# Last stage of a graph network: spreading the senders' values without diagonals, and the low rows of the table made by GpSimd

## The reference, cut to what matters

```python
def _L1_gnn_ref(x, edge, W, a):
    h = x @ W
    src, dst = (edge[0], edge[1])
    s = h @ a[:f_out]
    t = h @ a[f_out:]
    logit = s[src] + t[dst]
    e = jnp.exp(-jax.nn.leaky_relu(logit, ALPHA))
    rowsum = jax.ops.segment_sum(e, src, num_segments=n)
    msg = e[:, None] * h[dst]
    h_prime = jax.ops.segment_sum(msg, src, num_segments=n)
    h_prime = h_prime / rowsum[:, None]
    return jax.nn.relu(h_prime)
...
x = _layernorm(x + _L1_gnn_ref(x, edge_index, L1_gnn_W, L1_gnn_a), axis=-1)
```

## Time and profile before

| | |
|---|---|
| time, median of three runs | 2623.73 us (2621.55 to 2624.15) |
| time of the profiled execution | 2622.26 us |
| span of its instructions | 2620.5 us |
| busy: PE, DVE, ACT, POOL | 93%, 75%, 50%, 22% of the span |
| last stage: first DMA issue, end of the span | 1706.8 us, 2620.5 us |
| mean granted clock of PE | 0.972 |

### The profile page before, as it was taken

The page is one execution under the profiler, slowest core; times in us unless marked ns, Lnnn a source line. Parts: engine busy times, 40 slices in busy tenths (PEclk is TensorE's granted clock), DMA queues, the critical chain, the costliest instruction groups (busy, mean ns, idle before and its releaser), DMA issues. The chain is left out here.

```text
span 2620.5 us, 46932 instructions
## 1 busy us (share of the span) xinstructions
PE 2425.1 (93%) x16048; PEld 1966.7 (75%) x16048; DVE 1954.9 (75%) x3244; ACT 1318.5 (50%) x2190; POOL 578.7 (22%) x629
## 2 busy tenths in 40 slices
PE   3899969999999999959898889889999999999996
PEld 2566647777777777736565556579999999999996
DVE  5899966666666666637576566589999898989896
ACT  3222338888888888814433334355434334343432
POOL 4698960000000000024243324100001010101010
PEclk9999989999999999979999999989999999999998
DMA  3111102223223222250202111166464545454543
GB/s 99 36 46 44 44 18 120 117 106 132 106 109 129 106 121 117 106 173 29 71 29 71 57 57 43 57 149 145 94 124 90 117 89 124 89 121 89 120 92 71
DMA packets 405991, 239.92 MB, mean 92 GB/s; under 512 B 326288, under 2 KB 397584, under 8 KB 399568
## 3 DMA queue, kind: packets, MB, share of 16 engines
q1 hardware_dynamic: 397536, 228.12, 32.0%
q10 hardware_dynamic: 7056, 6.43, 0.7%
q0 software_dynamic: 1248, 3.41, 0.5%
HBM read 48.38 MB, written 110.84 MB: 61 GB/s over the span
## 5 line engine op out<-in xcount | busy, mean ns | idle before, releaser
L1792 PE MATMUL d_acc<-d_rows_high,d_weights_high 128*128 128x258 f32 x2401 | 682.8, 284 | 6.1 <-DVE d_weights_low L1668 6.1
L1793 PE MATMUL d_acc<-d_rows_low,d_weights_high 128*128 128x258 f32 x2401 | 678.6, 283 | 0.0
L1794 PE MATMUL d_acc<-d_rows_high,d_weights_low 128*128 128x258 f32 x2401 | 678.2, 282 | 0.0
L1422 PE MATMUL b_pagg<-x_parts,b_counts 128*128 128x512 f32 x2401 | 656.4, 410 | 0.5 <-ACT b_counts L1463 0.5
L1742 ACT CAST d_weights_high<-d_weights 128x896 fp32r<-128x896 f32 x343 | 323.4, 945 | 500.9 <-PE d_acc L1794 293.3
L1422 PEld LDWEIGHTS b_pagg<-x_parts,b_counts 128*128 128x128 f32 x2401 | 423.7, 189 | 74.4 <-ACT b_counts L1463 1.1
L1792 PEld LDWEIGHTS d_acc<-d_rows_high,d_weights_high 128*128 128x128 f32 x2401 | 455.3, 190 | 10.2 <-DVE d_weights_low L1668 6.0
L1793 PEld LDWEIGHTS d_acc<-d_rows_low,d_weights_high 128*128 128x128 f32 x2401 | 455.3, 190 | 2.2 <-issue 2.2
L1794 PEld LDWEIGHTS d_acc<-d_rows_high,d_weights_low 128*128 128x128 f32 x2401 | 455.1, 190 | 0.0
L1107 DVE TENSOR_TENSOR b_lo_hot<-b_nodes,b_ends 128x1024 bf16<-128x1024 f16 x392 | 270.9, 691 | 210.9 <-PE b_pcounts L1433 210.5
L1668 DVE TENSOR_TENSOR d_weights_low<-d_weights,d_weights_high 128x896 fp32r<-128x896 f32 x343 | 373.1, 1088 | 52.8 <-ACT d_weights_high L1742 51.2
(11 more groups left out here) (160 smaller groups left out, 2790.4 us busy)
## 6 DMA issues: line engine op xcount, KB each, us to landing
edge_counts<-b_counts SPq DMA_DIRECT2D x49, 1568.0 KB, 5.1
node_table<-u_table SPq DMA_DIRECT2D x7, 903.0 KB, 6.3
qx<-in_x SPq DMA_DIRECT2D x49, 128.0 KB, 2.0
x_table<-x_tile ACTq DMA_DIRECT2D x49, 128.0 KB, 1.7
agg<-b_sums SPq DMA_DIRECT2D x49, 128.0 KB, 4.5
u_x<-x_table SPq DMA_DIRECT2D x7, 896.0 KB, 8.2
u_agg<-agg SPq DMA_DIRECT2D x7, 896.0 KB, 10.1
u_x<-in_x SPq DMA_DIRECT2D x7, 896.0 KB, 5.1
```

Of the source, the lines that this page charges most:

```text
L1422: last = nc.tensor.matmul(pagg[:, o, :], ca[:, o, hi, :], x1_parts[:, hi].rearrange("p m d -> p (m d)"), start=(hi == 0), stop=(hi == TILE ...
L1792: nc.tensor.matmul(acc[:, r, 0:HT], a, high[:, t, :], start=(t == 0), stop=False)
L1793: nc.tensor.matmul(acc[:, r, 0:HT], a, low[:, t, :], start=False, stop=False)
L1794: return nc.tensor.matmul(acc[:, r, 0:HT], b, high[:, t, :], start=False, stop=(t == TILES - 1))
```

## The change

DVE no longer makes diagonals. The spread of four tiles of senders' values is now four matmuls of 128 columns: the stationary operand is one column of `st` repeated 128 times, the moving operand is the identity. PE no longer waits for DVE there, only for ACT to have kept the spread before.

`set_ones` and `rows_low` move from DVE to POOL. `rows_low` becomes two instructions: the staged row times `t_scale`, written in place, and then that minus `high`. The second waits for the first on the new semaphore `scaled`. POOL's queue holds all 49 rows ahead of its loop over the inverse roots. DVE's queue in the first group keeps `weigh` and `weights_low` alone.

```diff
@@ vector
-                    dve.wait_ge(ones_ready, 1)
-                    for q in range(FIRST):
-                        diagonals(q)
-                    set_ones(0)
-                    for m in range(ROWS_AHEAD - 1):
-                        rows_low(m)
...
                             if t >= 1:
                                 weights_low(J, t - 1)
-                            if not finish:
-                                if late_spread(t):
-                                    diagonals(late_spread(t))
-                                if t + ROWS_AHEAD < TILES and (t + ROWS_AHEAD) % GROUP == 0:
-                                    set_ones((t + ROWS_AHEAD) // GROUP)
-                                if t + ROWS_AHEAD - 1 < TILES:
-                                    rows_low(t + ROWS_AHEAD - 1)
@@ gpsimd
                     nc.gpsimd.memset(ones[:], 1.0).then_inc(ones_ready, 1)
+                    pool.wait_ge(ones_ready, 1)
+
+                    def set_ones(g):
+                        pool.wait_ge(tab_in[g % 2], 16 * (g // 2) + 16)
+                        nc.gpsimd.tensor_copy(staged[g % 2][:, :, D], ones[:, 0:GROUP]).then_inc(one_set, 1)
+
+                    def rows_low(m):
+
+                        row = staged[m // GROUP % 2][:, m % GROUP, :]
+                        pool.wait_ge(high_ready, m + 1)
+                        nc.gpsimd.tensor_tensor(row, row, t_scale[:, m:m + 1].broadcast_to([P, HT]), ALU.mult).then_inc(scaled, 1)
+                        pool.wait_ge(scaled, m + 1)
+                        nc.gpsimd.tensor_tensor(low[:, m, :], row, high[:, m, :], ALU.subtract).then_inc(low_ready, 1)
+
+                    set_ones(0)
+                    for m in range(TILES):
+                        if (m + ROWS_AHEAD) % GROUP == 0 and (m + ROWS_AHEAD) // GROUP < GROUPS:
+                            set_ones((m + ROWS_AHEAD) // GROUP)
+                        rows_low(m)
@@ tensor
                     def spread_sources(q):
-                        pe.wait_ge(diag_ready, q + 1)
                         if q >= 1:
                             pe.wait_ge(s_ready, q)
                         at = spread_cols(q)
-                        nc.tensor.matmul(acc[:, GROUP, 0:at.stop - at.start], ones[:], diag[:, q % 2, 0:at.stop - at.start],
-                                         start=True, stop=True).then_inc(spread, 1)
-
-                    pe.wait_ge(ones_ready, 1)
+                        for t in range(q * per, min(TILES, (q + 1) * per)):
+                            col = t % per * P
+                            last = nc.tensor.matmul(acc[:, GROUP, col:col + P], c["st"][:, t, 0:1].broadcast_to([P, P]), c["ident"][:],
+                                                    start=True, stop=True)
+                        last.then_inc(spread, 1)
+
```

More of the change, by code:

```diff
@@ L1486, in weigh_and_sum @@
         t_cap, t_scale = sb("d_t_cap", [P, TILES]), sb("d_t_scale", [P, TILES])
-        diag, ones = sb("d_diag", [P, 2, 512]), sb("d_ones", [P, P])
+        ones = sb("d_ones", [P, P])
         cnt = sb("d_counts", [P, GROUP, cols], F16)
@@ L1504, in weigh_and_sum @@
             kit.sem("d_" + s) for s in ("added", "stats", "mean", "var", "rstd", "ready"))
-        ones_ready, diag_ready, spread, s_ready, exp_t = (
-            kit.sem("d_" + s) for s in ("ones_ready", "diag_ready", "s_spread", "s_ready", "exp_t"))
-        one_set, high_ready, low_ready = (kit.sem("d_" + s) for s in ("one_set", "rows_high", "rows_low"))
+        spread, s_ready, exp_t = (kit.sem("d_" + s) for s in ("s_spread", "s_ready", "exp_t"))
+        ones_ready, one_set, high_ready, scaled, low_ready = (
+            kit.sem("d_" + s) for s in ("ones_ready", "one_set", "rows_high", "rows_scaled", "rows_low"))
         tab_in = [kit.sem(f"d_table_loaded{k}") for k in range(2)]
```

## The result

The changed kernel takes 2637.04 us (median of five runs, 2634.74 to 2639.23) against 2623.73 us for the kernel before (median of five, 2621.55 to 2624.59). The ratio is 1.0055, with a 95% interval of 1.0041 to 1.0068: slower by 13.3 us. The forecast was 2644 us, with a range of 2631 to 2662.

What follows compares the result with a forecast made beforehand. PE bounds the first group, DVE close behind. DVE's 101.0 + 95 x 0.54 = 152.3 us moves the group's end from 1852.0 to 1872.5, a 20.5 us loss: 2642.8 on the profiled execution, 2644.2 forecast, range 2631 to 2662.

Steps and rivals of the forecast that it cites:

- PE is the bound, DVE close behind: First group before the change: PE needs 2.52 us a tile, 5.90 for two with a spread; DVE about as much.
- The start, at most 1.2 us: Group's start: first `weigh` no earlier, first `weights_low` about 2.1 us behind it instead of 3.31; worth at most 1.2 us.
- The spreads on PE, taken at nothing: Four matmuls replacing one on PE: eight weight loads hide, a spread still costs 0.86 us, nothing added.
- the rival that they become PE's bound: Spreads' weight loads don't hide on PE: 12 us more than the main case, 2656 us; chance 0.05.
- POOL and DVE take turns: First group: each new POOL instruction waits for DVE's instruction in hand, then holds up the next; a tile takes 3.14 us.
- 0.54 us for each: DVE's loss per POOL row instruction in the first group; 95 of the 98 stand between DVE instructions.
- a multiply that holds DVE half as long: Low variant of the main case, from the multiply's repeated column: a tile takes 2.87 us, the kernel 2634 us.
- Seven blocks ahead, which covers a few us: SP's table-tile loads wait for `low_ready` with transposes behind them; their lead of seven blocks was said to cover a few us.
- POOL's rows hidden: Rival: PE stays the bound if a POOL instruction costs DVE under 0.23 us; 2622.5 us, not slower; chance 0.13.
- POOL holds DVE for its whole instruction: Rival: each POOL instruction costs DVE 0.725 us, 17.6 us more than the main case: 2662 us; chance 0.05.
- PE's clock falls for the whole group: Rival: PE's waits lower its clock, products 0.22 us apart in the first group; about 2735 us; chance 0.04.
- PE waits in nearly every tile: Sign in the first group: PE should wait for `weights_low` or the low rows in nearly every tile.

Runs made afterwards that it cites:

- the first experiment: The changed kernel with `set_ones` and `rows_low` put back into DVE's queue as one instruction, the spreads staying new: 2619.93 us, ratio 0.9984 against the kernel before.

## Why the prediction was right, and where it was off

**PE is the bound, DVE close behind: right.** With 23.6 us of rows kept and 10.7 us of diagonals taken from DVE, the first experiment's group is as long as before.

**The start, at most 1.2 us: nothing came of it.** The first `weigh` still waits for its transposed counts, as predicted. The first `weights_low` comes 1720.01 - 1717.09 = 2.9 us after it, not 2.1, since POOL already takes its turns there.

**The spreads on PE, taken at nothing: right.** 0.89 us for 0.86; the rival that they become PE's bound is refuted by the first experiment.

**POOL and DVE take turns: right, but 0.54 us for each was too much.** This is the mis-sized term. In the undisturbed tiles, 2.87 to 2.98 us, the cost is (2.92 - 2.06) / 2 = 0.43 us, and in all 35.6 us were added to DVE's lines instead of 51.3: by 0.43 that is 83 instructions' worth, not 95. In the trace 85 of POOL's 98 row instructions are in hand when a DVE instruction of the group starts; the others ran ahead of the group or while DVE stood. The prediction named a multiply that holds DVE half as long as the way to a tile of 2.87 us and to 2634 us. The tiles come close to that, but by another split. In the timeline above `weigh` lasts 1.50 us behind a multiply, 0.35 over its 1.15, and `weights_low` 1.63 behind a subtraction, 0.54 over its 1.09; around 1836 us, where the pairs lie the other way round, the multiply costs 0.41 and the subtraction 0.38. Alone the multiply is the shorter of the two, 0.61 us against 0.74; that its repeated column is the reason was not tried. The counts of turns bear the mechanism out: one for a row costs nothing in the whole, two cost about 10 us, three 38 us more, and with a second input in PSUM the collision is gone. (POOL's instruction in the earlier trace rows is L749, not the L747 of the earlier trace rows; its own median is 0.728 us, so nothing hangs on it.)

**"Seven blocks ahead, which covers a few us": the step that failed.** It looked at SP's loads as they stood, not at how late POOL would be by then. POOL lost its lead of three rows, SP waited 12.7 us ahead of the load of `xm` where it had waited 7.6 for DVE's rows, and the counts behind it came 6.5 us late. With the load moved the median is 3.6 us lower and the group 1.7 us shorter.

The two errors go against each other. Predicted were 157.2 us from the first `weigh` to the start of the last product; the turns took 15.7 us less, the late counts 7.1 us more, small differences on DVE about 1.3 more, and PE needed 6.7 us behind the end of the last `weights_low` at 1862.16 us instead of 4.9: about 151.7, and 151.8 were measured. That the time came as near to the forecast as it did is luck in part: with the load moved it is 2633.43 us, near the low end of the range. That PE waits in nearly every tile shows in its pace rather than in the list of waits: 358 products at 0.12 us fill 43.0 of the 48 us shown above, while the list has eight waits for weights in the whole group. A matmul's listed 0.28 us overlaps the next one's start by 0.16, so a pause becomes a listed wait only beyond that.

**The other rivals.** POOL's rows hidden: false with two instructions for a row, true with one. POOL holds DVE for its whole instruction, as the Trainium skill puts it (SBUF — State Buffer, section "SBUF: two separate sides", where this stands, ahead of the section that the prediction names): 0.43 us were lost for instructions that take 0.61 and 0.74 alone, so the trace agrees on who excludes whom, but the loss is shorter than the instruction. PE's clock falls for the whole group: false; it fell for 6.8 us behind DVE's stand.

## What to carry to other kernels

Before work goes to GpSimd because it has time, count the instructions of VectorE that read two SBUF tiles in the same stretch (here the diagonals, which read one, were held up too): the two engines took turns one for one here, so each GpSimd instruction had its price on VectorE (0.43 us), and GpSimd got no more turns than VectorE had instructions. Splitting one fused instruction into two on the other engine doubled that price here, while one instruction for each row fitted behind TensorE's pace, and a second input that lies in PSUM made the price vanish for that line. And where an engine's slack is measured in rows of lead, follow the queue behind every wait on its semaphore: one DMA issue with the next blocks behind it stopped VectorE for 6.5 us here.

## What the runs showed of the hardware

- A blocked GpSimd instruction paid a wait that its own size did not set: the copy of 128 x 7 ones takes 0.195 us alone and 1.06 us between DVE's instructions. The DVE instruction behind it kept its old length, 1.14 or 1.08 us.
- A DVE instruction with one SBUF tile as input collided too: the diagonals, a multiplication of an fp32 tile by a column, took 535 ns beside POOL and 285 without.
- Four matmuls of 128 columns with a repeated column as the stationary operand cost PE 0.89 us, one of 512 columns with a matrix of ones 0.86: the weight loads were hidden (eight of 0.189 us one after another would be 1.5 us).
- At two of the six changes from one group to the next PE stands for 2 to 3 us, and in some executions the granted clock falls to its lower level for 3.4 us behind that. The length of the stand does not settle it: the clock fell behind 2.08 us (changed kernel, up to 2116.88 us) and not behind 3.22 us (first experiment, up to 2348.26 us). Two windows of 3.2 us, just behind the start of the fourth group's products, show it in the kernel before and not in the first experiment:

```profile
2101.20:2104.40 3.20, 3.20 (x17) 3.20 (x16) 2.36 (x3) 0.00 (x0) 0.00 (x0) 0.50 0.60 110
```

```profile
2099.60:2102.80 3.20, 3.20 (x29) 3.20 (x28) 3.20 (x4) 0.81 (x1) 0.00 (x0) 1.00 0.87 107
```

  17 products instead of 29 is a loss of 12 x 0.12 = 1.4 us. The kernel before has two such stretches in its profiled execution and the first experiment none, and from the first group's last product to the seventh's the one takes 745.8 us and the other 742.7. That is about the 3.4 us between their medians. Over all ten profiled executions this part takes 741.4 to 742.7 us without such a stretch, 743.0 to 744.8 with one and 744.5 to 745.8 with two; the changed kernel has two as well. Whether the number belongs to the kernels or only to the profiled executions stays open.
